# Expert results added by the scatter into a running sum, and values projected per row block

## The chip, the cores and the metric

The kernel runs on one core of a Trainium2 chip. The metric is the device time of one execution in microseconds (us). The core has five engines that run their own instruction streams and meet at semaphores: PE (TensorE, matrix products), DVE (VectorE), ACT (ScalarE), POOL (GpSimd) and SP (SyncE, which here only issues DMAs). The profile lists PE's weight loads apart, as PEld. Sixteen DMA engines carry the transfers that the engines issue.

## What is computed

x has 8 batches of 512 rows of 256 numbers (float32). After a layernorm, two results are added to x:

```python
xn = _layernorm(x)                       # over the 256 columns, no scale
x = x + attention(xn) + ffn(xn)

# attention: 16 heads of 16, windows of 128 rows, stride 64; their outputs stand one
# behind the other and are cut to 512 rows, so four windows (320 rows) per batch count
qkv = xn @ w_qkv + b_qkv
ow = softmax(qw @ kw.T / 4) @ vw         # per window and head
o = ow.reshape(b, nw * 128, 256) @ w_out + b_out
return o[:, :512, :]

# ffn: each row goes to the 2 of 8 experts with the highest scores
topk_scores, topk_idx = top_k(xn @ gate_w.T, 2)
topk_probs = softmax(topk_scores)        # the row's two shares
h12 = xn @ w12[e].T
y = sum over the two experts of  share * ((silu(h1) * h2) @ w3[e].T)
```

## The kernel before

**Stages.** Times are those of the trace. From 0 to 53 x is loaded (L375, four DMAs), normalised into XN and stored to `xn_scratch` in DRAM (`store_xn`, L381), and transposed; the gates' scores and batch 0's projections are made. From 53 to 157.5 attention runs for batches 0 and 1 (EXTRA = 2), and beside it the routing: which row goes to which slot of which expert, and its two shares, kept in PW. From 157.5 to 513.5 the experts run over 71 tiles of 128 slots (SLOT_TILES). From 513.5 to the end attention runs for batches 2 to 7.

**Attention.** A batch has four windows of two units each, u = 0 to 7; a unit is 8 heads of one window. The work is pipelined over units. Each unit on PE: projections for the next batch (queries and keys of a row block in u = 0 to 3, into W_BANK; values of window n = u - 4 in u = 4 to 7, by `values`), the scores three units ahead, the `shifted` scores (L1399: KS by QALL, 8 products of 128x128 for 8 heads, in two halves of 4), `weighted` sums with VW, and every second unit `project`. ACT copies projections out of the bank (`take_part`, `take_values` L741, one copy of 128x256 per window), makes the exponentials (`exps`, L781), copies a row of shifts (`take_shift`, L776) and every second unit the window's sums and denominators (`sides`, L788, L789). DVE splits queries and keys into three bf16 levels, finds maxima (L964), takes the reciprocal of the denominators (L1122, once per window) and adds in `project` (L1132). POOL multiplies (`divide`, L595). SP stores the levels to `parts_scratch` and loads them in another layout (QS, KS); `begin(b)` holds these DMAs of a batch. XNT holds the next batch's transposed rows, loaded by `load_tokens`.

**Experts.** For a tile j POOL gathers 128 rows of `xn_scratch` (`gather`, L654, an indirect DMA into one of two buffers XS), PE transposes them (`tokens`, L1527) and multiplies, ACT copies the result YS (`take_y`, L893), and POOL scatters it to `ys_scratch`, a row of its own for each (token, choice) pair (`scatter`, L658). The weights lie in WALL, 384 KB per DMA (`load_experts`, L449, 4 DMAs per expert); those of experts 6 and 7 (LATE = 6) come last, when the slot map is done, and PE's and ACT's expert programs begin behind a wait for them (`late_in`, L899, L1520).

**Putting together.** After the experts WALL is free. Rows of x (`in_x`, XR) and the two results of each row (YG) are loaded batch by batch (`rest`, 1.5 MB in three DMAs); ACT multiplies each result by its share (`scale`, L796, 64 in all) and POOL adds three terms per tile of 128 rows (`combine`, L601 to L603). For batches 3 to 7 that is done for the batch at hand (`own`), ahead of `divide`, and `project` adds the sum instead of the bias; for batches 2, 0 and 1 it is done later, within batches 4, 5 and 6 (`later`), and `send_later` stores them. Batches 0 and 1's attention output waits in DRAM meanwhile (`keep`, L481, `rows_scratch`).

The order of all engines' work is written out by hand in loops over batches and units; nothing is scheduled by a planner. `c["W"]` and its like count the uses of a bank.

## Time and profile before

| | us |
|---|---|
| median of 3 runs | 712.34 |
| lowest, highest | 712.1, 715.86 |
| the profiled execution | 713.24 |
| its span, from the first to the last instruction | 711.5 |

The profile is of one execution. A line "busy" names engines by the time they execute something; PE's share includes pipelined matrix products whose ends are modelled. The chain of waits is followed back from the last instruction: at each step to what released it. Since the stages have different limits, a view of a stretch or of one engine's timeline tells more than the averages over the span.

### The profile page before, as it was taken

The numbers are of one execution on the slowest core, as the hardware profiler recorded it, in microseconds if no ns is written. First come the engines' busy times: TensorE is split into PE (matmuls) and PEld (weight loads), VectorE is DVE, ScalarE is ACT, GpSimd is POOL, SyncE is SP. The second block draws the span as 40 slices with busy tenths as digits, with TensorE's granted clock in tenths as the row PEclk, the third lists the DMA queues.
The fourth block names the chain that finished last, engine by engine and source line by source line (L and its number), as shares of the span: only waits on it lengthen the run. The fifth ranks groups of instructions, "written<-read, shape, count | busy, mean of one in ns | idle before, by whom it ended". The sixth has DMA issues, their size and how long they took to land.

```text
span 711.5 us, 17988 instructions
## 1 busy us (share of the span) xinstructions
PE 633.2 (89%) x5916; PEld 512.0 (72%) x5917; DVE 571.6 (80%) x906; ACT 513.7 (72%) x883; POOL 280.4 (39%) x330
## 2 busy tenths in 40 slices
PE   0786776978999999999999999999889899999995
PEld 0564554754888888888888888888767676666673
DVE  4958899975688888888888888888687979788884
ACT  4554477474687787787777777777667788888885
POOL 3000273031344444444444444444300336666654
PEclk9998788998999999999999999999999999999999
DMA  9895477581111111111111111112168687885840
GB/s 300 268 257 174 128 262 273 146 284 31 49 53 52 59 52 52 59 53 50 59 55 50 57 56 51 56 54 56 45 161 258 174 259 180 271 227 161 215 138 30
DMA packets 66384, 92.74 MB, mean 130 GB/s; under 512 B 6448, under 2 KB 53424, under 8 KB 66320
## 3 DMA queue, kind: packets, MB, share of 16 engines
q1 hardware_dynamic: 57904, 70.56, 33.3%
q0 software_dynamic: 6864, 18.75, 7.9%
q10 hardware_dynamic: 1568, 2.76, 1.2%
q8 instruction: 32, 0.52, 0.3%
q14 instruction: 16, 0.13, 0.1%
HBM read 59.06 MB, written 32.83 MB: 129 GB/s over the span
## 4 chain that ended last, share of the span: by engine, by line
PE 63%; DVE 14%; ACT 10%; issue 8%; DMA 2%; POOL 2%; ACTq 0%; SPq 0%; DVEq 0%; POOLq 0%
PE PS L1300 55%; PE PS L1549 4%; DVE SMALL L964 4%; ACT WORK L781 3%; DVE XN L1122 2%; PE PS L1527 2%; DVE WALL L958 2%; ACT QS L776 1%; DMA XN<-in_x 1%; DVE WORK L1033 1%; DVE WORK L1026 1%; POOL OTS L595 1%; ACT WORK L719 1%; DVE WALL L982 1%; DMA KS<-parts_scratch 1%
## 5 line engine op out<-in xcount | busy, mean ns | idle before, releaser
L367 DVE TENSOR_TENSOR WS<-WALL,WS 128x1024 fp32r<-128x1024 f32 x136 | 166.9, 1227 | 56.0 <-ACT WS L862 41.5
L1300 PE MATMUL PS<-WS,XTS 128*128 128x512 f32 x804 | 203.9, 402 | 0.0
L1300 PEld LDWEIGHTS PS<-WS,XTS 128*128 128x128 f32 x804 | 146.2, 189 | 30.5
L862 ACT ACTIVATE WS<-WALL 128x1024 fp32r x136 | 143.7, 1056 | 9.1 <-issue 0.3
L1300 PE MATMUL PS<-DOWN_HIGH,HTS 128*128 x568 | 108.3, 290 | 5.0 <-DVE DOWN_LOW L958 3.5
L595 POOL TENSOR_TENSOR OTS<-SIDE,XN 128x256 f32<-128x256 f32 x31 | 23.8, 768 | 209.2 <-DVE XN L1122 142.2
L1300 PEld LDWEIGHTS PS<-DOWN_HIGH,HTS 128*128 128x128 f32 x568 | 86.4, 190 | 5.5 <-issue 5.5
L964 DVE TENSOR_REDUCE SMALL<-PS 128x8 f32<-128x1024 f32 x64 | 77.5, 1211 | 12.6 <-PE PS L1300 12.4
L781 ACT ACTIVATE WORK<-PS 128x512 f32<-128x512 f32 x128 | 69.4, 594 | 24.8 <-PE PS L1300 21.4
L658 POOL DMA_INDIRECT ys_scratch<-SIDE,SIDX x36 | 43.8, 1215 | 97.0 <-ACT SIDE L893 97.0
L654 POOL DMA_INDIRECT XS<-xn_scratch,GIDX x72 | 70.4, 978 | 23.6 <-issue 21.6
L1300 PE MATMUL PS<-DOWN_LOW,HTS 128*128 x284 | 79.5, 280 | 0.0
L658 POOL DMA_INDIRECT ys_scratch<-OTS,SIDX x35 | 45.0, 1286 | 81.6 <-ACT OTS L893 81.6
L776 ACT ACTIVATE QS<-PS 16x1024 bf16<-16x1024 bf16 x64 | 65.1, 1017 | 3.4 <-PE PS L1396 1.9
L1300 PEld LDWEIGHTS PS<-KS,QS 96*128 96x128 bf16 x512 | 33.1, 101 | 31.5 <-DVE SMALL L964 24.2
L958 DVE TENSOR_TENSOR HTS<-PS,HTS 128x512 fp32r<-128x512 f32 x71 | 49.1, 692 | 7.2 <-ACT HTS L877 7.2
L1122 DVE RECIPROCAL XN<-XN 128x256 f32<-128x256 f32 x31 | 54.1, 1746 | 0.0
L1300 PEld LDWEIGHTS PS<-DOWN_LOW,HTS 128*128 128x128 f32 x284 | 53.9, 190 | 0.0
L1300 PE MATMUL PS<-KS,QS 96*128 96x128 bf16 x512 | 41.1, 225 | 12.6 <-DVE SMALL L964 12.3
L958 DVE TENSOR_TENSOR WORK<-WORK,PS 128x512 f32<-128x512 f32 x71 | 48.4, 681 | 3.9 <-PE PS L1300 3.9
L1300 PE MATMUL PS<-WORK,VW 128*32 128x128 f32 x1024 | 42.6, 285 | 5.2 <-ACT WORK L781 5.2
L1300 PE MATMUL PS<-WOUT,OTS 128*128 128x256 f32 x128 | 36.1, 405 | 11.7 <-POOL OTS L595 9.5
(148 smaller groups left out, 1094.8 us busy)
## 6 DMA issues: line engine op xcount, KB each, us to landing
WALL<-in_wexp SPq DMA_DIRECT2D x28, 384.0 KB, 7.1
WALL<-ys_scratch SPq DMA_DIRECT2D x16, 512.0 KB, 7.3
parts_scratch<-WORK SPq DMA_DIRECT2D x32, 240.0 KB, 2.5
QS<-parts_scratch SPq DMA_DIRECT2D x16, 480.0 KB, 4.6
XN<-in_x SPq DMA_DIRECT2D x4, 1024.0 KB, 12.1
xn_scratch<-XN SPq DMA_DIRECT2D x4, 1024.0 KB, 7.2
WALL<-in_x SPq DMA_DIRECT2D x8, 512.0 KB, 5.7
KS<-parts_scratch SPq DMA_DIRECT2D x16, 240.0 KB, 3.9
```

The lines of the kernel that those rows point to most:

```text
L367: eng.tensor_tensor(out=WS[:, 1 - k, half, 1], in0=weights, in1=WS[:, 1 - k, half, 0].bitcast(F32), op=ALU.subtract).then_inc(low_ready[ha ...
L595: pool.tensor_tensor(out=OTS[:].rearrange("p c n -> p (c n)"), in0=SIDE[:], in1=DENS, op=ALU.mult).then_inc(turned_ready, 1)
L654: pool.indirect_dma_start(XS[:, j % 2, :], None, xn_dram, bass.IndirectOffsetOnAxis(GIDX[:, j:j + 1], 0)).then_inc(xs_in[j % 2], 16)
L658: pool.indirect_dma_start(ys_dram, bass.IndirectOffsetOnAxis(SIDX[:, j:j + 1], 0), YS[j % 2], None).then_inc(y_out[j % 2], 16)
L776: act.activation(to, SHIFT_ROW.unsqueeze(1).to_broadcast([2 * HH, HH, WIN]), ACT.Copy).then_inc(t_free, 1)
L781: act.activation(PT[:, 2 * (u % 2) + q, :], ST_BANK[q], ACT.Exp, scale=SCALE).then_inc(probs_ready, 1)
L862: act.activation(WS[:, 1 - k, half, 0], weights, ACT.Copy).then_inc(high_ready[half], 1)
L958: return dve.tensor_tensor(out=o, in0=a, in1=b, op=op)
L964: return dve.tensor_reduce(out=o, in_=a, axis=AX_X, op=op, **kw)
L1122: dve.reciprocal(out=DENS, in_=DENS).then_inc(recip_ready, 1)
L1300: return pe.matmul(o, a, b, start=start, stop=stop)
L1549: last = pe.transpose(bank(6)[:, f * P:(f + 1) * P], HID[:, k, f * P:(f + 1) * P], IDF[:])
```

## The change

**Shares.** PW is laid out [128, 32, 2], and after making it DVE signals `shares_made`. ACT, in batch 0 at u = 5, stores it into two new columns of `xn_scratch`, whose rows now have 258 numbers. A gather so brings a row's two shares along; `take_map` makes a mask KIND (which of the two a slot is), and POOL picks the share by two small operations (`find_share`), two tiles ahead. `take_y` multiplies by it in its copy.

**The sum.** `sum_scratch` starts as a copy of x, made by eight DRAM-to-DRAM DMAs (`copy_x`): two behind the first loads of experts' weights, six ahead of the late ones. `scatter` adds to it, and each waits for the scatter before; the first waits for all copies. `keep` adds batches 0 and 1's attention output to it from POOL. After the experts `rest` loads 0.5 MB per batch; `own` adds the bias only, for all batches from 2 on; `scale`, `later`, `rows_back` and `send_later` are gone. Batches 0 and 1 go from `sum_scratch` to the output in two DMAs.

**Values.** They are projected once for row blocks of 128, 128 and 64 rows in u = 4, 5, 6 (the last into T_BANK); ACT copies them in six pieces to the four windows' places. Odd windows then hold their keys' rows with the halves swapped, so `shifted` of an odd window puts its two halves by two products of 64 columns.

```diff
+VBLOCKS = -(-SPAN // P)
+BLOCK_USES = 4 + VBLOCKS
+VTAKES = (((0, 0, P), (1, STRIDE, P)), ((2, 0, P), (1, 0, STRIDE)), ((3, STRIDE, P),), ((3, 0, STRIDE),))
...
+        xn_dram = nc.dram_tensor("xn_scratch", (B * L, ROW), F32, kind="Internal").ap()
+        sum_dram = nc.dram_tensor("sum_scratch", (DUMP_ROW + SLOT_TILES * P, D), F32, kind="Internal").ap()
...
+            def copy_x(b):
+                r = slice(b * L, (b + 1) * L)
+                sp.dma_start(sum_dram[r], x[r]).then_inc(x_copied[b], 16)
 
             def rest(b):
-
                 t = slice(b * TB, (b + 1) * TB)
-                sp.dma_start(XR[:, t, :], xv[:, t, :]).then_inc(rest_in[b], 16)
-                for k in range(2):
-                    sp.dma_start(YG[:, t, k, :], yv[:, t, k, :]).then_inc(rest_in[b], 16)
-
-            def rows_back(b):
-                t = slice(b * TB, (b + 1) * TB)
-                sp.dma_start(XN[:, t, :], rv[:, t, :]).then_inc(rows_in[b], 16)
-                rest(b)
+                sp.dma_start(XR[:, t, :], sv[:, t, :]).then_inc(rest_in[b], 16)
...
-            def keep(b):
-                sp.wait_ge(r_free, (b + 1) * NWIN + 1)
-                t = slice(b * TB, (b + 1) * TB)
-                sp.dma_start(rv[:, t, :], XN[:, t, :]).then_inc(rows_out, 16)
-
             begin(0)
             load_experts(FIRST_EXPERTS, EARLY - 1)
+            for b in range(EXTRA):
+                copy_x(b)
             sp.wait_ge(early_done, 1)
             load_tokens(1)
             load_experts(EARLY - 1, LATE)
             begin(1)
+            for b in range(EXTRA, B):
+                copy_x(b)
             sp.wait_ge(map_done, 1)
             load_experts(LATE, E)
-            keep(0)
-            load_tokens(2)
-            keep(1)
-            sp.wait_ge(rows_out, 16 * EXTRA)
+            load_tokens(EXTRA)
...
             for b in range(EXTRA, LAST):
                 begin(b)
                 rest(b + 1)
                 if b < LAST - 1:
                     load_tokens(b + 1)
-                if b + 2 in LATER:
-                    if LATER[b + 2] < EXTRA:
-                        rows_back(LATER[b + 2])
-                    else:
-                        rest(LATER[b + 2])
-                if b > OWN:
+                if b == EXTRA:
+                    for src in range(EXTRA):
+                        r = slice(src * L, (src + 1) * L)
+                        sp.dma_start(out[r], sum_dram[r]).then_inc(out_done, 16)
+                else:
                     send(b - 1)
...
-            def combine(t, first, ready):
-
-                total = XR[:, t, :]
-                link(pool.tensor_tensor(out=total, in0=total, in1=first, op=ALU.add))
-                link(pool.tensor_tensor(out=total, in0=total, in1=YG[:, t, 0, :], op=ALU.add))
-                pool.tensor_tensor(out=total, in0=total, in1=YG[:, t, 1, :], op=ALU.add).then_inc(ready, 1)
+            def keep(b):
+
+                pool.wait_ge(r_free, (b + 1) * NWIN + 1)
+                pool.wait_ge(x_copied[b], 16)
+                t = slice(b * TB, (b + 1) * TB)
+                pool.dma_start(sum_dram[0:B * L].rearrange("(t p) d -> p t d", p=P)[:, t, :], XN[:, t, :],
+                               accum_op=ALU.add).then_inc(rows_out[b], 16)
 
             def own(b, n):
-                pool.wait_ge(own_scaled, 2 * ((b - OWN) * TB + n + 1))
-                pool.wait_ge(rest_in[b], 48)
-                combine(b * TB + n, BOUT[:], own_ready)
-
-            def later(b, n):
-
-                pool.wait_ge(later_scaled, 2 * ((b - FIRST_LATER) * TB + n + 1))
-                src = LATER[b]
-                pool.wait_ge(rest_in[src], 48)
-                if src < EXTRA:
-                    pool.wait_ge(rows_in[src], 16)
-                else:
-                    pool.wait_ge(r_free, src * NWIN + n + 2)
-                combine(src * TB + n, XN[:, src * TB + n, :], later_ready)
+                pool.wait_ge(rest_in[b], 16)
+                t = b * TB + n
+                pool.tensor_tensor(out=XR[:, t, :], in0=XR[:, t, :], in1=BOUT[:], op=ALU.add).then_inc(own_ready, 1)
...
+            keep(0)
 
             def gather(j):
                 pool.indirect_dma_start(XS[:, j % 2, :], None, xn_dram,
                                         bass.IndirectOffsetOnAxis(GIDX[:, j:j + 1], 0)).then_inc(xs_in[j % 2], 16)
 
             def scatter(j):
-                pool.indirect_dma_start(ys_dram, bass.IndirectOffsetOnAxis(SIDX[:, j:j + 1], 0),
-                                        YS[j % 2], None).then_inc(y_out[j % 2], 16)
+                if j:
+                    pool.wait_ge(y_out[1 - j % 2], 16 * ((j + 1) // 2))
+                else:
+                    for b in range(B):
+                        pool.wait_ge(x_copied[b], 16)
+                    for b in range(EXTRA):
+                        pool.wait_ge(rows_out[b], 16)
+                pool.indirect_dma_start(sum_dram, bass.IndirectOffsetOnAxis(SIDX[:, j:j + 1], 0),
+                                        YS[j % 2], None, compute_op=ALU.add).then_inc(y_out[j % 2], 16)
+
+            def find_share(j):
+                k = j % 2
+                pool.wait_ge(xs_in[k], 16 * (j // 2 + 1))
+                link(pool.tensor_tensor(out=PAIR[:], in0=XS[:, k, D:ROW], in1=KIND[:, j, :], op=ALU.mult))
+                pool.tensor_tensor(out=SHARE[:, k:k + 1], in0=PAIR[:, 0:1], in1=PAIR[:, 1:2], op=ALU.add
+                                   ).then_inc(share_ready, 1)
+                pool.wait_ge(share_ready, j + 1)
 
             pool.wait_ge(map_done, 1)
             for blk in range(4):
                 pool.wait_ge(parts_out[blk], PARTS_OUT[blk // 2] * (EXTRA + 1))
+            pool.wait_ge(shares_out, 16)
             gather(0)
             gather(1)
             divide(6)
             divide(7)
+            find_share(0)
+            find_share(1)
             pool.wait_ge(xt_full, 1)
             gather(2)
...
+            keep(1)
             for j in range(SLOT_TILES):
                 if j + 3 < XS_TILES:
                     pool.wait_ge(xt_full, j + 2)
                     gather(j + 3)
                 pool.wait_ge(ys_ready, j + 2)
                 scatter(j)
+                if j + 2 < SLOT_TILES:
+                    find_share(j + 2)
...
-                    if b in LATER:
-                        later(b, n)
-                    if b >= OWN:
-                        own(b, n)
+                    own(b, n)
                     if b * NWIN + n < B * NWIN - 1:
...
-            def take_values(n, bk, full, ready):
+            def take_values(i, bk, full, ready):
                 act.wait_ge(full[0], full[1])
-                act.activation(values_of(n), values_in(bk), ACT.Copy).then_inc(ready, 1)
+                for n, lo, hi in VTAKES[i]:
+                    last = act.activation(values_of(n)[lo:hi], values_in(bk)[lo:hi], ACT.Copy)
+                last.then_inc(ready, 1)
...
-                    elif not last and u < UNITS - 1:
-                        take_values(u - 4, W_BANK[:, 0:D], (w_full, c["W"].add()), w_free)
-                    if b in LATER and u % 2 == 0:
-                        scale(LATER[b] * TB + u // 2, LATER[b], later_scaled)
-                    if b >= OWN and u % 2 == 1:
-                        scale(b * TB + u // 2, b, own_scaled)
+                    elif not last and u == 4:
+                        take_values(0, W_BANK[:, 0:D], (w_full, c["W"].add()), w_free)
+                    elif not last and u == UNITS - 2:
+                        take_values(1, W_BANK[:, 0:D], (w_full, c["W"].add()), block_taken)
                     if b == 0 and u == 1:
                         act.wait_ge(gap_ready, 2)
                         act.activation(E2, PA, ACT.Exp).then_inc(e2_ready, 1)
                         act.wait_ge(xn_out, 64)
+                    if b == 0 and u == 5:
+                        act.wait_ge(shares_made, 1)
+                        act.dma_start(xn_dram.rearrange("(t p) d -> p t d", p=P)[:, :, D:ROW], PW[:]
+                                      ).then_inc(shares_out, 16)
                     if u % 2 == 1:
                         if b == EXTRA and u == 1:
                             act.wait_ge(y_stored, 1)
                         sides()
                     if u == UNITS - 1 and not last:
-                        take_values(NWIN - 1, W_BANK[:, 0:D], (w_full, c["W"].add()), w_free)
+                        take_values(2, W_BANK[:, 0:D], (w_full, c["W"].now()), w_free)
+                        take_values(3, T_BANK[:, 0:D], (w_full, c["W"].add()), w_free)
...
-                    act.activation(YS[k], bank(7)[:, 0:D], ACT.Copy).then_inc(ys_ready, 1)
+                    act.wait_ge(share_ready, j + 1)
+                    act.activation(YS[k], bank(7)[:, 0:D], ACT.Copy, scale=SHARE[:, k:k + 1]).then_inc(ys_ready, 1)
...
-                link(ts(MB, hi, float(NT), float(B * L), ALU.is_gt, ALU.mult))
-                link(tt(MB, MA, MB, ALU.subtract))
+                link(ts(KIND[:, :, 0], hi, float(NT), None, ALU.is_le, ALU.bypass))
+                link(ts(KIND[:, :, 1], hi, float(NT), None, ALU.is_gt, ALU.bypass))
+                link(dve.scalar_tensor_tensor(out=MB, in0=KIND[:, :, 1], scalar=-float(B * L), in1=MA, op0=ALU.mult,
+                                              op1=ALU.add))
...
+                rows = min(P, SPAN - n * P)
                 for ch in range(NC_D):
-                    last = mm(o, xt[:, ch, n * STRIDE:n * STRIDE + WIN], WQKV[:, ch, 2 * D:3 * D],
+                    last = mm(o[0:rows], xt[:, ch, n * P:n * P + rows], WQKV[:, ch, 2 * D:3 * D],
                               ch == 0, ch == NC_D - 1)
...
-                        last = mm(o, KS[:, par, half * HH + h, w], QALL[0:DEEP, par, half * HH + h, w])
+                        moving = QALL[0:DEEP, par, half * HH + h, w]
+                        if n % 2 == 0:
+                            last = mm(o, KS[:, par, half * HH + h, w], moving)
+                        else:
+                            for part in range(2):
+                                at = (n + 1 - part) * STRIDE
+                                last = mm(o[part * STRIDE:(part + 1) * STRIDE],
+                                          KS[:, par, half * HH + h, at:at + STRIDE], moving)
```

ACT's order in batch 0, around the operations of u = 5. Before:

```order
L808 ACTIVATE XN<-XN,WALL 128x512 [waits apart]
L776 ACTIVATE QS<-PS 16x8x128 [waits t_full]
L743 ACTIVATE VW<-PS 128x2x8x16 [waits w_full]
L788 ACTIVATE SIDE<-PS 128x256 [waits turned_ready,o_full]
L789 ACTIVATE XN<-PS 128x256
L781 ACTIVATE WORK<-PS 128x512 [waits sides_ready,st_full]
```

and now:

```order
L796 ACTIVATE XN<-XN,WALL 128x512 [waits apart]
L769 ACTIVATE QS<-PS 16x8x128 [waits t_full]
L815 DMA xn_scratch<-PW 128x32x2 [waits shares_made]
L781 ACTIVATE SIDE<-PS 128x256 [waits turned_ready,o_full]
L782 ACTIVATE XN<-PS 128x256
L774 ACTIVATE WORK<-PS 128x512 [waits sides_ready,st_full]
```

The DMA of PW stands between `take_shift` and `sides`.

SP's order from the end of batch 1's loads to the expert tiles. Before, the late weights follow the last KS loads directly, with the stores of `keep` behind them:

```order
L412 DMA KS<-parts_scratch 48x2560 [waits parts_out3]
L412 DMA KS<-parts_scratch 32x2560
L412 DMA KS<-parts_scratch 16x2560
L449 DMA WALL<-in_wexp 128x768 [waits map_done]
L449 DMA WALL<-in_wexp 128x768 x7
L481 DMA rows_scratch<-XN 128x4x256 [waits r_free]
L429 DMA WORK<-xt_scratch 128x640 [waits w_full]
L481 DMA rows_scratch<-XN 128x4x256 [waits r_free]
```

and now:

```order
L410 DMA KS<-parts_scratch 48x2560 [waits parts_out3]
L410 DMA KS<-parts_scratch 32x2560
L410 DMA KS<-parts_scratch 16x2560
L451 DMA sum_scratch<-in_x 16x8192 x6
L447 DMA WALL<-in_wexp 128x768 [waits map_done]
L447 DMA WALL<-in_wexp 128x768 x7
L427 DMA WORK<-xt_scratch 128x640 [waits w_full]
```

Six copies stand ahead of the late weights, and `keep` has left SP.

POOL's order at the start of the expert tiles. Before (L595 is `divide`, L654 `gather`, L658 `scatter`):

```order
L654 DMA XS<-xn_scratch,GIDX 128x256 [waits parts_out2,parts_out1,parts_out3,parts_out0,map_done]
L654 DMA XS<-xn_scratch,GIDX 128x256
L595 TENSOR_TENSOR OTS<-SIDE,XN 128x256 [waits r_full,recip_ready,sides_ready] x2
L654 DMA XS<-xn_scratch,GIDX 128x256 [waits xt_full] x2
L658 DMA ys_scratch<-SIDE,SIDX 17280x256 [waits ys_ready]
L654 DMA XS<-xn_scratch,GIDX 128x256 [waits xt_full]
L658 DMA ys_scratch<-OTS,SIDX 17280x256 [waits ys_ready]
L654 DMA XS<-xn_scratch,GIDX 128x256 [waits xt_full]
```

and now (L577 is `divide`, L585 `keep`, L627 `gather`, L638 `scatter`, L644 and L645 `find_share`):

```order
L585 DMA sum_scratch<-XN 128x4x256 [waits x_copied0,r_free]
L627 DMA XS<-xn_scratch,GIDX 128x258 [waits parts_out2,parts_out3,parts_out1,shares_out,parts_out0,map_done]
L627 DMA XS<-xn_scratch,GIDX 128x258
L577 TENSOR_TENSOR OTS<-SIDE,XN 128x256 [waits r_full,recip_ready,sides_ready] x2
L644 TENSOR_TENSOR PAIR<-XS,KIND 128x2 [waits xs_in0]
L645 TENSOR_TENSOR SHARE<-PAIR 128x1 [waits pool_step]
L644 TENSOR_TENSOR PAIR<-XS,KIND 128x2 [waits xs_in1,share_ready]
L645 TENSOR_TENSOR SHARE<-PAIR 128x1 [waits pool_step]
L627 DMA XS<-xn_scratch,GIDX 128x258 [waits xt_full,share_ready]
L585 DMA sum_scratch<-XN 128x4x256 [waits x_copied1,r_free]
L627 DMA XS<-xn_scratch,GIDX 128x258 [waits xt_full]
L638 DMA sum_scratch<-SIDE,SIDX 13184x256 [waits x_copied5,x_copied4,x_copied6,x_copied3,x_copied7,x_copied2,rows_out0,x_copied1,rows_out1,x_copied0,ys_ready]
```

Accumulating stores and the shares' operations have come between the gathers, and a scatter now waits for the one before.

## Rows read from the trace of the kernel before

**Rows 1.** The page: busy time (part 1) and shares of the chain of waits (part 4)

```profile
PE 633.2 (89%) x5916; PEld 512.0 (72%) x5917; DVE 571.6 (80%) x906; ACT 513.7 (72%) x883; POOL 280.4 (39%) x330
...
PE 63%; DVE 14%; ACT 10%; issue 8%; DMA 2%; POOL 2%; ACTq 0%; SPq 0%; DVEq 0%; POOLq 0%
```

**Rows 2.** Stretches: us, busy us (operations) by engine, granted clock, DMA share, GB/s

```profile
105.00:107.00 2.00, 0.95 (x10) 0.79 (x11) 2.00 (x3) 1.86 (x4) 2.00 (x4) 1.00 1.04 340
145.00:149.00 4.00, 4.00 (x59) 3.23 (x58) 2.27 (x5) 2.93 (x6) 1.31 (x2) 1.00 1.02 393
153.00:155.00 2.00, 0.00 (x0) 0.00 (x0) 1.98 (x2) 1.96 (x3) 0.00 (x0) 1.00 1.02 378
200.00:250.00 50.00, 50.00 (x311) 43.85 (x309) 41.73 (x52) 38.79 (x63) 23.29 (x21) 1.00 0.15 52
```

**Rows 3.** The load of x at the start: four DMAs of 1024 pieces

```profile
L375 SPq DMA_DIRECT2D XN<-in_x x4: 441/2160/4292, 0.8 to 6.3; - x4
...
DMA to landing us min/median/max: 9.1/12.1/14.0
```

**Rows 4.** Last two late expert loads, issued at 144.5 and 145.0: time to landing

```profile
DMA to landing us min/median/max: 8.6/9.3/10.1
```

**Rows 5.** Chain of waits, batch 1 into expert tiles: start, length, operation

```profile
156.28 1.15 PE PS L1300 x4
...
157.47 0.53 PE PS L1527 x2
```

**Rows 6.** Costliest groups: busy us, mean ns | idle before, its releaser

```profile
L1300 PE MATMUL PS<-DOWN_HIGH,HTS 128*128 x568 | 108.3, 290 | 5.0 <-DVE DOWN_LOW L958 3.5
```

**Rows 7.** POOL in the expert loop: start, length, operation, idle before it

```profile
302.34 1.27 POOL L658 DMA_INDIRECT ys_scratch<-SIDE,SIDX  x1 [2.31 <-ACT SIDE L893]
303.91 0.97 POOL L654 DMA_INDIRECT XS<-xn_scratch,GIDX  x1 [0.30 <-issue]
...
308.76 0.97 POOL L654 DMA_INDIRECT XS<-xn_scratch,GIDX  x1 [0.30 <-issue]
```

**Rows 8.** Scatters of expert results from 300 to 313: issue to landing

```profile
DMA to landing us min/median/max: 2.4/2.7/2.7
```

**Rows 9.** DVE in batch 2

```profile
527.16 1.75 DVE L1122 RECIPROCAL XN<-XN 128x256 f32<-128x256 f32 x1
...
529.98 0.49 DVE L958 TENSOR_TENSOR WORK<-WORK 128x320 bf16<-128x320 f32 x1
...
533.94 1.75 DVE L1122 RECIPROCAL XN<-XN 128x256 f32<-128x256 f32 x1
```

**Rows 10.** DVE in batch 3

```profile
550.69 1.75 DVE L1122 RECIPROCAL XN<-XN 128x256 f32<-128x256 f32 x1
...
559.82 1.75 DVE L1122 RECIPROCAL XN<-XN 128x256 f32<-128x256 f32 x1
...
562.64 0.90 DVE L958 TENSOR_TENSOR WORK<-WORK 128x320 bf16<-128x320 f32 x1
...
567.01 1.74 DVE L1122 RECIPROCAL XN<-XN 128x256 f32<-128x256 f32 x1
```

**Rows 11.** DVE in batch 4: its first three reciprocals

```profile
584.01 1.75 DVE L1122 RECIPROCAL XN<-XN 128x256 f32<-128x256 f32 x1
...
593.60 1.75 DVE L1122 RECIPROCAL XN<-XN 128x256 f32<-128x256 f32 x1
...
601.20 1.75 DVE L1122 RECIPROCAL XN<-XN 128x256 f32<-128x256 f32 x1
```

**Rows 12.** ACT in the last unit of batch 2: the copy of values

```profile
544.75 0.38 ACT L743 ACTIVATE VW<-PS 128x256 f32<-128x256 f32 x1
```

**Rows 13.** PE's weight loads in batch 3, last window: a DMA wait

```profile
572.21 0.45 PEld L1300 LDWEIGHTS PS<-KS,QS 96*128 96x128 bf16 x8 [0.39 <-DMA KS<-parts_scratch]
```

**Rows 14.** ACT's scaling of loaded expert results, all of it

```profile
L796 ACT ACTIVATE WALL<-WALL,PW x64: 491/497/510, 551.1 to 703.9; 128x256 f32<-128x256 f32 x64
```

**Rows 15.** Chain of waits from 680 to the end: its shares by line

```profile
by line: ACT WORK L781 26.9%; PE PS L1300 24.8%; ACT QS L776 9.5%; issue 8.9%; ACT WALL L796 5.6%; ACT SIDE L788 4.8%; DVE XN L1130 3.9%; ACT XN L789 3.5%; DVE XN L958 2.2%; ACT VW L743 1.2%; ACTq L791 0.2%; DVEq L1137 0.1%
```

83 lines of the change are left out of this document (36 added, 47 removed).

## The prediction

> **What bounds the kernel now.** I read the page first [rows 1]. PE is busy 89% of the span and leads the chain of waits with 63%, but that is an average over stages with different limits. So the second view is the table of stretches [rows 2], and within a stage the timelines. In the expert tiles (157.5 to 513.5) PE is busy 50.00 of 50.00 us at full clock [rows 2] and everything else has room: POOL idles 2.31 us before a scatter [rows 7]. One tile takes 4.85 us (gathers at 303.91 and 308.76 [rows 7]). In attention batch 0 it is ACT and DVE: 1.86 and 2.00 of 2 us busy while PE works 0.95, in the stretch from 105 to 107 [rows 2]. From batch 2 on a chain through all engines sets the pace, window by window; its beat is read from the starts of L1122 on DVE [rows 9 to 11]. Between these stages stands one transfer, the late experts' weights: from 145 to 155 the DMA engines are full (1.02 shares, 378 to 393 GB/s [rows 2]).
>
> The sum is made on the profiled execution, 713.24 us for a span of 711.5; it lies 0.9 above the median 712.34, which comes off at the end. Edits within 0.5% (3.6 us) are about what a measurement of this kernel can tell from none.
>
> **The six copies ahead of the late weights.** Before, the last two late loads were issued at 144.5 and 145.0 and landed 8.6 and 10.1 us later [rows 4], so at 155.1. PE ends batch 1 at 157.43 and starts its first expert operation at 157.47 [rows 5]; that operation's sequencer waits for all late weights first, which cost nothing with 2.4 us to spare. Now six copies of x (3.15 MB) are issued on SP before those loads. At the 378 to 393 GB/s that the engines carry there [rows 2] they take 8.0 to 8.3 us, so the weights land at about 163.3 and PE starts 5.8 us late. Above that stands keep(0): issued behind the weights before, it may now be served ahead of them, 0.52 MB or 1.3 us, so 7.1. If DRAM-to-DRAM pieces move at half that rate it is 14; if the engines serve both queues side by side and copies finish last, below zero is excluded and it may be 0. I take **+6.5**. PE's start passes on whole: what follows is PE's own work, then its 3.5 us wait for DVE's DOWN_LOW [rows 6], and DVE makes those after `hidden(0)`, which needs PE. Nothing that batch 1 gains before this point survives it.
>
> **The shares' way out.** ACT, in batch 0's unit 5 (near 105), now issues one DMA of 4096 pieces of 8 bytes (128 x 32). No such DMA is in the trace. The nearest rows are the loads of x: four issues of 1024 pieces [rows 3]; the first two go in at once (0.44 and about 0.6 us), one takes 4.29, and each lands within 14.0 us of its issue. I read it as a queue that takes some 2000 pieces and holds the issuing engine for the rest until pieces have drained. Here half of 4096, so 128 on each of 16 engines, must drain with ACT held. With 1 KB pieces the queue moved 4096 of them in some 12 us, 256 per engine, so 47 ns for each. What 8 bytes take lies between nothing and that; I take a little over half, 27 ns, since some of the 47 must be fixed: 128 x 27 = **+3.5**. ACT stands on the limiting chain here [rows 2], so it counts whole. The lower end is 0.4 (the cheapest issue [rows 3]); the upper end follows if the pieces take turns with the early expert weights, with the engines at 1.04 shares from 105 on [rows 2]: then 128 pieces at 47 ns plus as much for each neighbour, 12 us.
> The Trainium skill, "DMA: Bandwidth & Descriptors", Specifications, says that below 512 B the DMA engine does a read-modify-write; it speaks against 8-byte shares, and by it the hold would lie nearer the upper end, the sum some 8 us higher. No row here has such small pieces.
>
> **The map.** `take_map` does 8 DVE operations for 7; the nearest row is an addition of 0.49 us on a tile four times as wide [rows 9], at least 0.1 remains: **+0.2**, on batch 1's DVE chain, partly absorbed by the wait above.
>
> **Expert tiles.** POOL gets two tiny operations per tile and `take_y` a wait for them. POOL idles 2.31 us per tile before the scatter [rows 7] and the shares are found two tiles ahead, so PE stays the limit. The scale itself rides on an ACT operation that is there anyway. New is the scatter's wait for the one before: issue to landing is 2.4 to 2.7 us for plain stores [rows 8]. An accumulating one must also read 128 KB; at one more transfer of that size (a gather's own length, 0.97 us of issue [rows 7] and about as much of flight) I estimate 3.5 to 4.3 us from issue to landing. That is under the period of 4.85, by 0.5 to 1.3. So **0**, with POOL's `gather(j+4)` queued behind the scatter's wait but not needed for a whole tile. The 8 bytes more in a gathered row of 1 KB cost nothing, since the gather is three tiles ahead.
> The Trainium skill, "DMA: Bandwidth & Descriptors", section "Anatomy of one DMA — SWDGE (gpsimd) path", gives 2.0 us fixed and the bytes at 436 GB/s, 2.3 us for 128 KB; the trace's 2.4 to 2.7 agrees. By it a second pass over the bytes adds only 0.3, and the wait would never bind; nothing in the sum changes.
>
> **Values.** Three row blocks replace four windows on PE. In batches 0 to 6 PE has four 128x256 products fewer in unit 7, none of them on the limiting chain, and ACT makes six copies for four. The copies: full ones take 0.38 us each [rows 12]. In batch 0 ACT limits: three more operations among the units (one partial) give 2 to 3 x 0.35, **+1.0**; in batch 1 it is absorbed. In batches 2 to 6 unit 7 has one more copy on the way sides, values, exps, shift, part, DVE: +0.33 each, below. The odd windows' `shifted` doubles its products (8 more of 64 columns per half). Eight weight loads take 0.45 us [rows 13], and PE waits 0.39 us there for KS from DRAM anyway, so 0 to 0.1. If halves in different columns run side by side, 0.
> The Trainium skill, "TensorEngine Tiling (Array Packing)", Key Properties, has tiles load weights and multiply in parallel; by that it is 0, by the row alone at most 0.45 in the two last units, 0.5 us per batch if DMA ceased to be late.
>
> **Stage 2, batches 2 to 7.** ACT's 64 scalings (0.497 us [rows 14]) go, and POOL adds one tile for three. From the reciprocals: window 0 to 1 takes 9.13 in batch 3 [rows 10] and 9.59 in batch 4 [rows 11], window 1 to 2 takes 6.78 in batch 2 [rows 9], 7.19 in batch 3, 7.60 in batch 4 (and in 5 and 6). The difference is contention of POOL's additions with DVE: one WORK addition takes 0.49 in batch 2 and 0.90 in batch 3 [rows 9, 10]. After, `own` runs once, right behind `divide`, in all batches from 2 on. So batch 2 rises to 7.19 (+0.41) and gets the copy (+0.33): +0.74. Batch 3: +0.33. Batches 4 and 5: -0.46 - 0.41 + 0.33 = -0.54 each. Batch 6 the same without most of the copy's charge, since batch 7 has no values to take: -0.87. In batch 7 ACT limits; L796 has 5.6% of the chain's last 32 us [rows 15], 1.8 us, of which the next limit (PE, 24.8%) takes back a little: -1.5. Sum 0.74 + 0.33 - 1.08 - 0.87 - 1.5 = **-2.4**. Bounds: +1 if nothing but batch 7 gains, -8 if contention leaves altogether. The loads fall from 1.5 MB to 0.5 MB per batch; none was waited for.
>
> **The sum.** 713.24 + 6.5 + 3.5 + 0.2 + 0 + 1.0 - 2.4 = 722.04; less 0.9: **721.1 us**.
>
> **The rivals.**
> - *Shares' issue is cheap* (0.4): 718.0. For it: the two first loads issued in 0.44 and 0.6 [rows 3]. Against: twice as many pieces as these together.
> - *Shares held among the expert loads* (12 us): 729.6. For it: DMA 1.04 busy from 105 [rows 2].
> - *The accumulating scatter is slower than a tile*: from 4.85 us on each of 71 tiles waits for the one before; at 5.5 it is 71 x 0.65 = 46 us, so 767. Against: 2.4 to 2.7 now [rows 8].
> - *The other side, faster*: ACT's scalings were on stage 2's path more than the chain of one execution tells. They are 64 x 0.497 = 32 us busy [rows 14]. The costs come to 11.2, so the kernel is faster by over 0.5% once more than 14.7 us of these 32 come back; at 19, it is 704.5. Against: ACT idles in most units there, and DVE's share of the beat doesn't change.
> - *The change's cost does not appear*: the copies are served beside the weights (0) and the issue is cheap (0.4): 713.24 + 1.6 - 2.4 - 0.9 = 711.5, no difference.
>
> **How the numbers follow.** Forecast 0.42 (716 to 726), cheap issue 0.15, held long 0.12, slow scatter 0.08, faster 0.13, no cost 0.10. Faster 0.13, same 0.14, slower 0.73, since a part of the cheap issue's range reaches under 715.9. For 8 in 10 the range leaves out the slow scatter and most of the faster case: 707 to 734.
>
> **What would show it.** In the changed profile: PE's first L1527 near 164 with a wait for a WALL load; ACT's DMA at L815 with 3 to 5 us between its neighbours; 4.85 us between gathers, and scatters landing under it; the second interval of batch 2 at 7.2, batch 4's first at 9.1; in batch 7 no L796. It would be wrong if scatters land later than 4.85, or if stage 2 sheds far more than 2.4.

## The result and the profile after

The changed kernel takes 728.8 us (median of 4 runs, 727.0 to 730.1) where the kernel before took 713.4 (four runs beside it, 712.1 to 715.9). The ratio is 1.021, with a 95% interval from 1.017 to 1.025: slower, by 1.7 to 2.5%. The forecast was 721.1 with a range of 707 to 734. The profiled execution has 729.2 us and a span of 727.5, 16.0 more than the 711.5 of before, and the rest of this text accounts for these 16.0.

The page of the changed kernel, busy times and the chain's shares; they answer to [rows 1]:

```profile
PE 636.5 (87%) x6140; PEld 507.8 (70%) x6141; DVE 569.2 (78%) x907; ACT 496.3 (68%) x835; POOL 346.0 (48%) x402
...
PE 59%; DVE 15%; ACT 10%; DMA 7%; issue 5%; POOL 3%; SPq 2%; ACTq 0%; DVEq 0%; POOLq 0%
```

PE has 3.3 us more to do and ACT 17 less, and yet the span grew: in the chain DMA rose from 2% to 7%. Where, the timelines tell. Set beside each other at five points of the program and at its end they give this table (starts of the same operation, us):

| | before | after | added in the stretch |
|---|---|---|---|
| DVE's last reciprocal of batch 1 | 153.36 | 153.69 | 0.3 |
| PE's first expert operation | 157.47 | 167.29 | 9.5 |
| ACT's copy of the first expert result | 173.98 | 183.89 | 0.1 |
| ACT's copy of the last (71st) expert result | 513.28 | 526.88 | 3.7 |
| DVE's first reciprocal of batch 2 | 527.16 | 540.75 | 0.0 |
| end of the span | 711.5 | 727.5 | 2.4 |

**The wait for the late weights.** The chain of waits of the changed kernel from 150 to 182; it answers to [rows 5]:

```profile
151.06 15.78 DMA WALL<-in_wexp
...
167.29 0.67 PE PS L1532 x2
```

The last load of the late experts' weights was issued at 151.06 and landed 15.8 us later. Before, the last one was issued at 145.0 and took 10.1 [rows 4]. Ahead of the weights the issue of the six copies held SP for 5.0 us, from 141.96 on.

**The shares' way out.** ACT's one DMA of 4096 pieces, from the view of its line:

```profile
L815 ACTq DMA_DIRECT2D xn_scratch<-PW x1: 393/393/393, 94.6 to 94.6; - x1
...
DMA to landing us min/median/max: 26.7/26.7/26.7
```

Its issue took 0.39 us; nothing was held. It stood at 94.6, not near 105 as the prediction read it. It landed 26.7 us later, and nobody waited for that.

**The expert tiles.** POOL's timeline in the loop (start, length, operation, idle before it); it answers to [rows 7]:

```profile
220.90 1.60 POOL L638 DMA_INDIRECT sum_scratch<-OTS,SIDX  x1 [0.30 <-issue]
221.96 1.56 POOL L644 TENSOR_TENSOR PAIR<-XS,KIND 128x2 f32<-128x2 f32 x1
223.61 0.19 POOL L645 TENSOR_TENSOR SHARE<-PAIR 128x1 f32<-128x1 f32 x1
224.30 1.00 POOL L627 DMA_INDIRECT XS<-xn_scratch,GIDX  x1 [0.49 <-POOL SHARE L645]
225.66 1.69 POOL L638 DMA_INDIRECT sum_scratch<-SIDE,SIDX  x1 [0.36 <-ACT SIDE L885]
```

POOL was idle for 2.3 us ahead of each scatter [rows 7]; now the gaps are 0.3 to 0.7 us, and POOL is busy for 39.9 of the 50 us from 200 to 250, where it was 23.3 [rows 2]. (The records of a scatter and of PAIR behind it overlap by some 0.5 us, so these lengths are rough.) The product PAIR of two columns takes 1.6 us here, but 0.20 where POOL is otherwise idle (at 162.0). The end of the loop on POOL:

```profile
524.51 1.58 POOL L638 DMA_INDIRECT sum_scratch<-OTS,SIDX  x1 [2.53 <-ACT OTS L885]
529.09 1.55 POOL L638 DMA_INDIRECT sum_scratch<-SIDE,SIDX  x1 [2.99 <-DMA sum_scratch<-OTS,SIDX]
```

The last scatter waited 2.99 us for the one before, which so took 4.6 us from issue to landing. Plain ones took 2.4 to 2.7 [rows 8].

**Attention from batch 2.** The reciprocals, as in [rows 9 to 11]. The first four here are those of batch 2's four windows (the last of them runs in batch 3's part of the program):

```profile
540.75 1.75 DVE L1116 RECIPROCAL XN<-XN 128x256 f32<-128x256 f32 x1
...
547.93 1.74 DVE L1116 RECIPROCAL XN<-XN 128x256 f32<-128x256 f32 x1
...
557.77 1.75 DVE L1116 RECIPROCAL XN<-XN 128x256 f32<-128x256 f32 x1
...
568.10 1.74 DVE L1116 RECIPROCAL XN<-XN 128x256 f32<-128x256 f32 x1
...
577.23 1.74 DVE L1116 RECIPROCAL XN<-XN 128x256 f32<-128x256 f32 x1
...
584.41 1.75 DVE L1116 RECIPROCAL XN<-XN 128x256 f32<-128x256 f32 x1
```

The steps are 7.18, 9.84, 10.33, 9.13 and 7.18. Before they were 6.78, 7.32, 9.43, 9.13 and 7.19. So batch 2 lost 3.8 us: 0.4, 2.5 and 0.9 in its three steps. In the step of 9.84 PE waits for KS from DRAM (timeline of its weight loads; it answers to [rows 13]):

```profile
555.50 0.45 PEld L1296 LDWEIGHTS PS<-KS,QS 96*128 96x128 bf16 x8 [2.65 <-DMA KS<-parts_scratch]
```

The step behind it has a part that belongs to no operation. From 557.1 to 560.5, right behind this wait, PE's granted clock is at its lower level, 1.2 GHz; from 530 to 557.1 and from 560.5 on it is 1.00. The row gives stretch, busy us (operations) by engine, granted clock, DMA share and GB/s:

```profile
557.10:560.50 3.40, 3.40 (x53) 2.83 (x53) 3.33 (x5) 2.10 (x3) 0.84 (x2) 0.50 0.40 159
```

The kernel before has no such stretch from batch 2 on until its last microsecond. In the profiled executions below with the same attention code, this third step is 10.2 to 10.3 where a stretch of 3.4 us at the lower clock lies at its start or just ahead of it (three others, with second steps of 9.9 to 10.9), and 9.8 where none does (four, with second steps of 7.8 to 8.9). Without the values part the second step is as long, 9.87, the clock stays at 1.00, and the third step is 9.43, as in that kernel's other batches. So I put 0.5 of the 0.9 down to the clock and 0.4 to the step's own work; no run sets the clock by itself.

From the reciprocal at 568.10 on, the changed kernel takes 159.4 us, before 160.8: here it gains 1.4.

### The profile page after: what moved, and what is told of

Its sections match the earlier page's. It is cut to its first block, busy times and chain, and to the rows that moved or that the text cites. A ratio compares the mean times of both kernels' runs of the same rounds, so it can differ in the third digit from the quotient of the medians.

```text
span 727.5 us, 18605 instructions
## 1 busy us (share of the span) xinstructions
PE 636.5 (87%) x6140; PEld 507.8 (70%) x6141; DVE 569.2 (78%) x907; ACT 496.3 (68%) x835; POOL 346.0 (48%) x402
## 4 chain that ended last, share of the span: by engine, by line
PE 59%; DVE 15%; ACT 10%; DMA 7%; issue 5%; POOL 3%; SPq 2%; ACTq 0%; DVEq 0%; POOLq 0%
PE PS L1296 52%; PE PS L1554 4%; DVE SMALL L957 4%; DVE XN L1116 3%; ACT WORK L774 2%; PE PS L1532 2%; DMA WALL<-in_wexp 2%; DVE WALL L951 2%; DMA KS<-parts_scratch 1%; DMA XN<-in_x 1%; DMA parts_scratch<-WORK 1%; ACT QS L769 1%; DVE WORK L1026 1%; DMA XS<-xn_scratch,GIDX 1%; DVE WORK L1019 1%
## 5 line engine op out<-in xcount | busy, mean ns | idle before, releaser
L577 POOL TENSOR_TENSOR OTS<-SIDE,XN 128x256 f32<-128x256 f32 x31 | 23.8, 768 | 259.9 <-DVE XN L1116 247.2
L1296 PE MATMUL PS<-DOWN_HIGH,HTS 128*128 x568 | 110.3, 293 | 5.0 <-DVE DOWN_LOW L951 3.5
L644 POOL TENSOR_TENSOR PAIR<-XS,KIND 128x2 f32<-128x2 f32 x71 | 108.0, 1522 | 5.8 <-DMA XS<-xn_scratch,GIDX 5.8
L627 POOL DMA_INDIRECT XS<-xn_scratch,GIDX x72 | 72.8, 1011 | 41.1 <-POOL SHARE L645 34.8
L638 POOL DMA_INDIRECT sum_scratch<-SIDE,SIDX x36 | 59.7, 1660 | 29.9 <-ACT SIDE L885 25.6
L638 POOL DMA_INDIRECT sum_scratch<-OTS,SIDX x35 | 58.3, 1665 | 18.1 <-ACT OTS L885 16.1
```

The source lines that it names most:

```text
L627: pool.indirect_dma_start(XS[:, j % 2, :], None, xn_dram, bass.IndirectOffsetOnAxis(GIDX[:, j:j + 1], 0)).then_inc(xs_in[j % 2], 16)
L638: pool.indirect_dma_start(sum_dram, bass.IndirectOffsetOnAxis(SIDX[:, j:j + 1], 0), YS[j % 2], None, compute_op=ALU.add).then_inc(y_out[j ...
L644: link(pool.tensor_tensor(out=PAIR[:], in0=XS[:, k, D:ROW], in1=KIND[:, j, :], op=ALU.mult))
L1296: return pe.matmul(o, a, b, start=start, stop=stop)
```

## The experiments

All were compared with the kernel before on the same chip, which took 712.8 to 713.7 there; the changed kernel was not run beside them, so differences to its 728.8 are good to about 1 us. Where a span or a step is told, it is that of the profiled execution. Profiled starts of the same point differ by up to 2.1 us between kernels that are alike up to there (the first reciprocal at 77.1 to 79.1), so stretches are better compared than starts.

### The copies and the accumulating store

The first two kernels move one of two suspects each, the third both.

Copies behind the late weights:

```diff
-            for b in range(EXTRA, B):
-                copy_x(b)
             sp.wait_ge(map_done, 1)
             load_experts(LATE, E)
+            for b in range(EXTRA, B):
+                copy_x(b)
```

> The changed kernel with its six copies of x issued behind the late experts' weights instead of ahead of them. The changed kernel's PE starts its first expert operation at 167.3 us, 9.8 later than before. Theory: 5.8 of these are the six copies (8.2 us of transfer less 2.4 of slack) and 4 are the accumulating store of batch 0's rows, which shares the queues' time with the weights. Then this kernel starts the experts near 158 to 161 (the accumulating store is still in the way) and takes about 7 to 9 us less than the changed kernel, 720 to 722. Rival: only the copies cost, moving at half the rate of a load, and the accumulating store nothing: start at 157.8, 719. If the wait was not what the copies caused, the time stays at 728 to 729.

Measured: 725.9 us, ratio 1.017 (1.014 to 1.020), 2.9 under the changed kernel and not the 7 to 9 expected. The weights are no longer what PE waits for, yet its first expert operation starts at 161.9 and the second pair at 165.0 (PE's weight loads):

```profile
161.91 0.29 PEld L1532 LDWEIGHTS PS<-IDF,XS 128*128 128x128 f32 x2 [3.02 <-issue]
165.00 0.29 PEld L1532 LDWEIGHTS PS<-IDF,XS 128*128 128x128 f32 x2 [2.79 <-DMA XS<-xn_scratch,GIDX]
```

The wait is now for the gathers. They stand on POOL's queue behind the accumulating store of batch 0's rows, issued at 145.1 and landed at 159.9; the second gather was on its way for 16.6 us (chain of waits), where the gathers of before took 6.2 and 6.6 beside the same weights:

```profile
148.38 16.57 DMA XS<-xn_scratch,GIDX
```

Whether the store delays them by its place in the queue or by its traffic, no run tells apart.

The store moved, the copies left where they are:

```diff
             for w in range(3, 6):
                 divide(w)
-            keep(0)
...
             gather(2)
+            keep(0)
             keep(1)
```

> The changed kernel with batch 0's accumulating store moved on POOL from ahead of the first gather to behind the third, beside batch 1's. Theory (the store takes 4 of the 9.8 us): PE's first expert operation at about 163.3 and the kernel at 724 to 725. Rival (the copies alone cost, at half rate): still at 167 and 728 to 729.

Measured: 724.9, ratio 1.015 (1.011 to 1.018), as expected; the four runs lie from 722.8 to 728.5, and the profiled one is the slowest of them. PE starts the experts at 165.15, 2.1 earlier than in the changed kernel, half of what the theory gave the store:

```profile
151.57 13.13 DMA WALL<-in_wexp
...
165.15 0.68 PE PS L1532 x2
```

Both moves:

> Both moves at once: copies behind the late weights, batch 0's accumulating store behind the third gather. Both theories: PE's first expert operation at 157.8 as before the change, and 719 to 720. If moving them only shifts the cost (first scatter waits for the copies, exact part of the experts waits for the stores), the experts' first results come late: ACT's first result after 175, and 722 or more.

Measured: 721.5, ratio 1.011 (1.008 to 1.015), span 718.7, between the theory's 719 to 720 and the rival's 722. PE's first expert operation is back at its old place:

```profile
157.47 1.12 PE L1532 MATMUL PS<-IDF,XS 128*128 128x128 f32 x4
```

So the 9.8 us are the copies and the store together. With the store alone moved 7.7 us of wait remain, with the copies alone moved 4.5, and only both moves free PE. (Counted from batch 1's last reciprocal, which comes 0.5 and 0.9 us later in these two profiles than in the changed kernel, it is 6.8 and 3.2 of 9.5.) The first expert result comes at 181.8 and 181.5 in these two, against 174.0 before; with the copies alone moved, PE waits again, until 165.0, for the second gather.

Of the 9.8 us, 8.5 arrive at the first expert result (16.5 us after PE's start before, 17.9 here). The other 1.4 lie on PE: ahead of the first products with DOWN_HIGH it reads the tile's expert number from EJ, and this one read took 1.67 us where it took 0.31 before. DVE's DOWN_LOW was ready as early as before (170.2). PE's reads from 165 to 176, before and here (ns, min/median/max):

```profile
L1578 PEldq TENSOR_LOAD <-EJ x3: 297/301/313, 170.3 to 173.6; - x3
...
L1583 PEldq TENSOR_LOAD <-EJ x3: 301/301/1667, 170.2 to 175.0; - x3
```

Why it was slow once, no run shows. And PE's granted clock was at its lower level for 6.8 us from 171.2 on, 2.6 of them behind the first result, where before it was 3.4 and 0.8. That lengthens the step to the second result, 6.87 us here, 5.93 before and 6.16 in the changed kernel. Over all fourteen profiled executions this step grows with the time at the lower clock in it, from 5.56 with none to 6.87 with 2.6 us, by 0.5 us for each.

### The values

Undone in the changed kernel (four products and copies per batch, undivided products in odd windows):

```diff
-                    elif not last and u == 4:
-                        take_values(0, W_BANK[:, 0:D], (w_full, c["W"].add()), w_free)
-                    elif not last and u == UNITS - 2:
-                        take_values(1, W_BANK[:, 0:D], (w_full, c["W"].add()), block_taken)
+                    elif not last and u < UNITS - 1:
+                        take_values(u - 4, W_BANK[:, 0:D], (w_full, c["W"].add()), w_free)
...
-                        if n % 2 == 0:
-                            last = mm(o, KS[:, par, half * HH + h, w], moving)
-                        else:
-                            for part in range(2):
-                                at = (n + 1 - part) * STRIDE
-                                last = mm(o[part * STRIDE:(part + 1) * STRIDE],
-                                          KS[:, par, half * HH + h, at:at + STRIDE], moving)
+                        last = mm(o, KS[:, par, half * HH + h, w], QALL[0:DEEP, par, half * HH + h, w])
```

> The changed kernel with values projected per window again (four products, four copies, undivided products in the odd windows), all else as changed. Theory: the values part costs one ACT copy in each of the seventh units of batches 2 to 6, +0.33 each, and 0.1 in one interval per batch; undone it gives 2 us back, 726 to 727, and the longest interval between reciprocals falls from 9.80 to 9.45. Rival: PE's doubled small products cost more, up to 0.9 per odd unit pair, 4 to 5 us in all: 724. Other rival: projecting three blocks helps PE and undoing it loses 1: 730.

Measured: 724.6, ratio 1.016 (1.013 to 1.019), 4.2 under the changed kernel. From the first reciprocal of batch 2 to the end it takes 183.2 us, the changed kernel 186.7. Two steps of each batch are shorter, 9.80 became 9.42, and 7.58 became 7.32, so the small products cost more than the theory gave them, as the first rival has it, though not 0.9. (0.5 of the 3.5 us is batch 2's third step, where the clock didn't fall here.) DVE's reciprocals:

```profile
582.16 1.74 DVE L1108 RECIPROCAL XN<-XN 128x256 f32<-128x256 f32 x1
...
589.48 1.74 DVE L1108 RECIPROCAL XN<-XN 128x256 f32<-128x256 f32 x1
...
598.90 1.75 DVE L1108 RECIPROCAL XN<-XN 128x256 f32<-128x256 f32 x1
```

The values part alone, in the kernel before:

> The kernel before with only the values part of the change (three row blocks, six copies, divided products in odd windows). Undoing this part in the changed kernel gave 4 us back (728.8 to 724.6; by the intervals between reciprocals 0.38 in one and 0.26 in another of each batch). Theory: it costs the same alone, +2.5 to +4: 715.5 to 717.5. Rival: in the kernel before ACT's scalings already delay unit 7, so the additional copy is hidden, and only the divided products show: +1 or less, 714.

Measured: 717.1 against 713.1, ratio 1.0048 (1.0031 to 1.0066), 4.0 us by the medians; span 715.9, +4.4. The theory holds and the rival falls: the additional copy isn't hidden by ACT's scalings. The steps from a batch's third to its fourth reciprocal, 9.43 to 9.52 before, became 9.81 to 9.94.

One more thing showed in the kernel without the values part. The step between the third and fourth reciprocal of the kernel is 13.95 us there, 12.56 in the changed one and before. PE waits for batch 1's rows (weight loads):

```profile
109.03 0.44 PEld L1288 LDWEIGHTS PS<-WORK,WQKV 128*128 128x128 f32 x2 [2.90 <-DMA WORK<-xt_scratch]
```

With per-window values PE is done with the rows of the batch before one unit later, so their load is issued later, and two copies of x then stand ahead of it. The values part made room for copies that the sum part brought.

### The expert loop

Both kernels of this part compute something else. The first leaves out POOL's two operations that find a share, from the third tile on, and scales with the first two tiles' shares:

```diff
                 scatter(j)
-                if j + 2 < SLOT_TILES:
-                    find_share(j + 2)
...
-                    act.wait_ge(share_ready, j + 1)
```

> The changed kernel with the two POOL operations that find a tile's share left out from the third tile on; results are scaled by the first two tiles' shares, so each row's experts are weighted wrongly. In the changed kernel ACT's results run from 183.9 to 526.9, 343.0 us for 70 tiles, before 339.3; in the last seven tiles PE waits 0.2 to 0.7 for a gather. Theory: these two operations (1.6 and 0.2 us, the first waiting for DVE's hold of the memory port) fill POOL's tile, gathers come late in the last tiles and every second tile is 0.08 longer. Without them 339.5 to 340.5 and 3 us less, 725 to 726. Rival: the accumulating scatter's traffic slows PE's weight loads and its wait delays the gathers: 343 stays, 728 to 729.

The second stores where the changed kernel adds, with all waits kept:

```diff
-                                        YS[j % 2], None, compute_op=ALU.add).then_inc(y_out[j % 2], 16)
+                                        YS[j % 2], None).then_inc(y_out[j % 2], 16)
```

> The changed kernel with the scatter storing plainly instead of adding (a row keeps the last result written, so the sums are wrong); its waits stay. Theory: an adding scatter takes about 4.6 us to landing (seen for the last but one, 524.51 to 529.09), a plain one 2.7; the loop doesn't feel it, 343 us from first to last result as in the changed kernel, but the last scatter no longer waits 3.0 us, the experts' end comes 3 to 4 us earlier for SP, and the second interval between reciprocals in batch 2 falls from 9.84 towards 7.6 to 8: 725 to 727. Rival: the adding scatter is what lengthens the loop: 340 us and 723 or less.

Measured: 727.5 (ratio 1.020, 1.017 to 1.024) and 725.5 (1.017, 1.015 to 1.020). What the loop did, from the starts of ACT's copies of the results:

| kernel | first to last result | mean of tiles 10 to 60 | last seven full tiles |
|---|---|---|---|
| before | 339.3 | 4.840 | 33.79 |
| changed | 343.0 | 4.873 | 35.21 |
| shares left out | 342.4 | 4.873 | 34.03 |
| plain scatter | 341.1 | 4.873 | 33.98 |
| values undone | 342.7 | 4.873 | 34.82 |
| values alone | 339.2 | 4.840 | 33.80 |

Two parts must be told apart. The last seven tiles lose 1.2 us because gathers come late; that is POOL's doing, and either experiment takes it away. PE's waits from 488 to 527 in the changed kernel (us in total, times, longest); in the two others there is no such row on XS:

```profile
PEld PS L1532 <- DMA XS<-xn_scratch,GIDX: 2.2, 5, 0.7
```

The other part, 0.033 us per tile or 2.3 in all, is untouched by both and by the values: neither theory nor rival holds for it. It lies in PE's own products of the second layer (costliest groups from 200 to 500, before and after):

```profile
L1300 PE MATMUL PS<-DOWN_HIGH,HTS 128*128 x496 | 93.6, 288 | 0.0
...
L1300 PE MATMUL PS<-DOWN_LOW,HTS 128*128 x248 | 68.9, 278 | 0.0
```

```profile
L1296 PE MATMUL PS<-DOWN_HIGH,HTS 128*128 x490 | 94.4, 291 | 0.0
...
L1296 PE MATMUL PS<-DOWN_LOW,HTS 128*128 x245 | 68.9, 281 | 0.0
```

Twelve of them at about 3 ns more make up the 0.033; the clock is 1.00 in both. The traces narrow the cause. The products' lengths come in two patterns, and both kernels have both. The kernel before runs its fourth and fifth tile in the longer one, 4.87 us apart, and stays in the shorter one, at 4.84, from the sixth on. The changed kernel has the shorter one in its third tile and again in tiles 66, 67 and 70, where gathers come late, and the longer one in nearly all others. Before from 188.5 to 198.2 and from 198.2 to 500, then changed from 506.1 to 508 (ns, min/median/max):

```profile
L1300 PE MATMUL PS<-DOWN_LOW,HTS x8: 281/281/283, 188.9 to 194.8; 128*128 x8
...
L1300 PE MATMUL PS<-DOWN_LOW,HTS x252: 276/277/282, 198.6 to 499.7; 128*128 x126
...
L1296 PE MATMUL PS<-DOWN_LOW,HTS x4: 276/278/280, 506.5 to 507.5; 128*128 x4
```

So gathered rows of 1032 bytes and another place in memory are not enough to lengthen a product: these three tiles have both. What decides in which pattern a loop stays is open.

The plain scatter's span is 4.9 us shorter: 0.3 ahead of the first result, 1.9 in the experts (1.2 in the last tiles, 0.6 ahead of the second result) and 2.7 behind them. Of these, the 0.6 and another 0.5 us in batch 2's third step are places where the clock was at its lower level in the changed kernel and not here. No run sets the clock by itself, so what brought that about is open. POOL at the end of its loop (compare the 2.99 us of wait above):

```profile
522.36 0.99 POOL L638 DMA_INDIRECT sum_scratch<-OTS,SIDX  x1 [3.65 <-ACT OTS L885]
525.51 0.96 POOL L638 DMA_INDIRECT sum_scratch<-SIDE,SIDX  x1 [2.17 <-ACT SIDE L885]
```

The last scatter waits only for its data, and the second step of batch 2 is 7.84 instead of 9.84. Where the shares are left out, the last tiles give their 1.2 back too, but that step is 10.88, and the kernel gains only 1.3 us by the medians, not the 3 expected.

### Who makes batch 2 wait

```diff
-                    outs(b + 1, half)
+                    if b != EXTRA or half:
+                        outs(b + 1, half)
...
+            sp.wait_ge(probs_ready, 2 * UNITS * EXTRA + 2)
+            outs(EXTRA + 1, 0)
             sp.wait_ge(y_stored, 1)
```

> The changed kernel with SP issuing the first half of batch 3's stores ahead of its wait for the last scatter, instead of behind it. Theory: batch 2's long second interval (9.84 against 7.32 before; PE waits 2.65 us for KS) comes from SP standing at that wait 3 us longer than before, so that the stores bunch with the next loads. Here it falls to 7.6 to 8 and the time by 2, 726 to 727. Rival: the transfers themselves (rows of the sum loaded by SP at the same time) are the cause: 9.8 stays, 728 to 729.

Measured: 728.3 (ratio 1.020, 1.018 to 1.023), only 0.5 less, within what runs differ by. The step fell to 8.69, not to 7.6 to 8: the first stores ahead of the wait give 1.15 us of the 2.5. (The third step fell too, from 10.33 to 9.82; the clock stayed at 1.00.) SP in the changed kernel:

```profile
533.13 0.56 SPq L486 DMA_DIRECT2D KS<-KS  x1
533.73 0.58 SPq L455 DMA_DIRECT2D WALL<-sum_scratch  x1
534.41 2.24 SPq L394 DMA_DIRECT2D parts_scratch<-WORK  x3
...
544.49 0.36 SPq L398 DMA_DIRECT2D parts_scratch<-WORK  x1
...
548.89 2.23 SPq L410 DMA_DIRECT2D KS<-parts_scratch  x3
```

SP stands until 533.13 for the last scatter (6.25 us after the last result; before 3.2: 513.28 to 516.47). Its stores then bunch with the loads that follow, and the one issued at 544.49 takes 4.4 us to land. With the plain scatter, SP is free 3 us earlier and the step is 7.84; so the cause is the accumulating scatter's late end, of which the order on SP passes on a part.

### Versions that were meant to be faster

All four repairs at once (copies and store behind, values undone, stores first; the edits are those shown above):

> The changed kernel with the copies behind the late weights, batch 0's accumulating store behind the third gather, values as before the change, and batch 3's first stores ahead of SP's wait. If the four repairs add up: 728.8 - 7.3 - 3.8 - 2 = 715.7, still 3 above the kernel before, the rest being the experts' stage. If the last overlaps with the first (batch 2's interval is already shorter without the copies), 717.

Measured: 717.8 against 713.7, ratio 1.0061 (1.0043 to 1.0080). The experts' stage still costs 3.1 us, the wait for batch 1's rows 1.8.

The share moved from ACT's copy to a product on DVE, alone in the changed kernel, to test what lengthens the tile:

```diff
-                    act.wait_ge(share_ready, j + 1)
-                    act.activation(YS[k], bank(7)[:, 0:D], ACT.Copy, scale=SHARE[:, k:k + 1]).then_inc(ys_ready, 1)
+                    act.activation(YS[k], bank(7)[:, 0:D], ACT.Copy).then_inc(ys_ready, 1)
...
-                    tt(HID[:, k, :], HID[:, k, :], bank(2 * k + 1), ALU.mult).then_inc(hid_done, 1)
+                    dve.wait_ge(share_ready, j + 1)
+                    dve.scalar_tensor_tensor(out=HID[:, k, :], in0=HID[:, k, :], scalar=SHARE[:, k:k + 1],
+                                             in1=bank(2 * k + 1), op0=ALU.mult, op1=ALU.mult).then_inc(hid_done, 1)
```

> The changed kernel with the share applied on DVE, in the product of the two halves of the hidden layer (a scalar as a third operand of an operation that is there anyway), and ACT's copy of the result unscaled again. The tile takes 4.873 us with or without POOL's share operations or the adding scatter, before 4.840. Theory: ACT's scaled copy (0.475 instead of 0.385 us) holds the result's bank longer and PE's next products in it wait a little every second tile: here 4.840 and 2.3 us less. Rival: rows of 1032 instead of 1024 bytes, or the additional load on memory, slow PE's weight loads: 4.873 stays. If DVE's three-operand form is much slower, the tile grows above 4.88.

Measured: 743.0, ratio 1.041 (1.039 to 1.043). The tile takes 5.13 us, for a reason that no theory had: DVE needs the share a stage earlier than ACT did, and POOL finds it behind the scatter, which waits for the result before. PE, DVE and POOL now stand in one ring (DVE's timeline):

```profile
302.78 0.75 DVE L1247 SCALAR_TENSOR_TENSOR WORK<-WORK,SHARE,PS 128x512 f32<-128x512 f32 x1 [0.44 <-POOL SHARE L645]
```

It doesn't settle the 0.033, since PE was not the limit in it. Both patterns of the products' lengths are mixed throughout its loop (DOWN_LOW 279 ns in the mean), with rows of 1032 bytes and the adding scatter in place. That fits with the theory that ACT's scaled copy has a part in it, but doesn't show it.

> The combined kernel of 717.8 with four further edits: all eight copies of x behind the late weights (two of them stood ahead of the load of batch 1's rows, and the interval from the third to the fourth reciprocal was 14.4 instead of 12.6), both accumulating stores of attention rows behind the fourth gather, the share applied on DVE, and found by one POOL operation (share times sign plus mask) instead of two. If all add up: -1.5, -1.3, -2.3 and -0.7 to -1.4: 711 to 712, 2 under the kernel before. If the scaled copy is not what lengthens the tile, 713.5 to 714.5.

Measured: 723.2, ratio 1.014 (1.012 to 1.016). The share on DVE spoiled it (tile 5.01). Its other edits did what they were for: the step between third and fourth reciprocal is 12.56 again, the first expert result comes at 175.1, and from the last result to the end it takes 194.7 us, where the kernel before takes 198.2.

The last version takes the share back to ACT, finds it ahead of the scatter, and has PE add the bias instead of POOL:

```diff
+                if biased:
+                    mm(R_BANK[:, 0:D], IDF[:], BOUT[:], True, False)
                 pe.wait_ge(turned_ready, c["R"].now() + 1)
```

> The kernel of 723.2 with the share applied again in ACT's copy of the result (applied on DVE, the tile waited for POOL's share and grew to 5.01 us), the share found ahead of the scatter instead of behind it, and POOL's addition of the bias gone from attention: PE adds it, as one more product of the identity with the bias in the projection's bank, ahead of its wait for POOL. Theory: first result at 175.1 as there, tile 4.87 (342 us for the experts), and without POOL's addition the interval from the first to the second reciprocal of a batch falls from 7.19 to 6.78, since DVE then never waits for POOL: 2.5 us over six batches. Sum: 721.0 - 9.0 - 2.5 = 709.5 in the profiled span, 711 to 712 in time, 1 to 2 under the kernel before. Rival: the 7.19 has another cause and stays: 714. If the share ahead of the scatter holds the scatters back, the tile grows: 716 or more.

Measured: 715.1 (11 runs) against 713.2 (16), ratio 1.0029 (1.0013 to 1.0045). The tile is 4.87 and the last tiles have no late gather, but from the first to the last result it takes 343.0 us, not 342: the step from the second to the third is 6.51 where it was 5.47. The step between the first two reciprocals of a batch is 6.78 in batches 2 to 6, as expected, so the 0.41 was POOL's addition against DVE:

```profile
531.08 1.75 DVE L1108 RECIPROCAL XN<-XN 128x256 f32<-128x256 f32 x1
...
533.90 0.49 DVE L943 TENSOR_TENSOR WORK<-WORK 128x320 bf16<-128x320 f32 x1
...
537.86 1.75 DVE L1108 RECIPROCAL XN<-XN 128x256 f32<-128x256 f32 x1
...
546.47 1.75 DVE L1108 RECIPROCAL XN<-XN 128x256 f32<-128x256 f32 x1
```

But the next step grew, from 7.32 (values undone, and in the version before this one) to 7.75, and batch 7's four steps from 23.2 to 24.2 in sum, and they took back more than that: from the first reciprocal of batch 2 to the end it takes 183.0 us, where the version before takes 181.1. PE's additional product is the one edit that adds work there; it was not tried alone. No version here beats the kernel before.

## Why the prediction was right, and where it wasn't

The direction and the place of the largest term were right: it is the wait for the late weights, as said, and 728.8 lies in the range. But it lies outside the 716 to 726 that the forecast itself covers, and in part the errors cancel, which is luck. The nearest number, 729.6, belonged to a rival whose mechanism (ACT held for 12 us by the shares) is not there at all. The sum came to +8.8 on the profiled execution and 16.0 were measured. By its terms:

- **Late weights: +6.5 forecast, 9.5 measured.** The mechanism was right, the size not. The step that failed took the queue's last landing at 163.3 by adding the copies' 8.2 us, at 378 to 393 GB/s, to the landing before, with keep(0) at most 1.3 on top. The store alone cost 2.1, and copies and weights without it landed at 164.7: from 142 to there the engines moved 333 GB/s in the mean (before, 349 from 142 to 155.1). What the step didn't have at all is that an accumulating store holds back the gathers issued behind it on POOL's queue. It is hidden in the changed kernel, since the weights are later still, and shows once they are not (4.5 us of wait).
- **Shares' issue on ACT: +3.5 forecast, 0 measured.** The reading of [rows 3] was wrong: a limit in pieces, taken from loads of 1 KB pieces, doesn't hold for this store. The landing took 26.7 us, but nothing waits for it. The Trainium skill, in "DMA: Bandwidth & Descriptors", Specifications, has the DMA engine do a read-modify-write below 512 bytes. The long landing of the 8-byte pieces doesn't speak against that; that it would hold the engine which issues them was the prediction's own step, and 0.39 us of issue contradict it.
- **Copies in batch 0 and the map: +1.2 forecast, 0.3 measured** at batch 1's last reciprocal. The two copies of x ahead of the load of batch 1's rows have no term; they cost nothing only because of the values part (1.4 us without it), which is luck.
- **Experts: 0 forecast, +3.7 measured.** The rival of the slow scatter didn't come: 4.6 us to landing, just above the estimate of 3.5 to 4.3 and under the period of 4.85. What failed is "POOL idles 2.31 us per tile", counted as room for two tiny operations. An adding scatter costs POOL 1.65 us of its own instead of 1.0 to 1.3, and the operation behind it 1.6 instead of 0.2, so the room was gone, which cost 1.2 us in the last tiles. The 2.3 us of slower products had no term, and why the loop stays in their longer pattern is open. The prediction weighed there the Trainium skill, "DMA: Bandwidth & Descriptors", section "Anatomy of one DMA — SWDGE (gpsimd) path". An estimate from its figures, with the bytes counted twice, is 2.6 us to landing for the adding scatter; the trace has 4.6, and the measurement decides.
- **The end of the experts: not in the sum.** The wait between scatters was priced per tile, where it is hidden, and not for the last one, where it isn't: 3.0 us there, 2.5 of them at the end of the chain in batch 2.
- **Attention from batch 2: -2.4 forecast, +2.4 measured.** The terms by POOL's contention were right to 0.05 (9.59 to 9.14, 7.60 to 7.19, 6.78 to 7.18). The values part was priced at 0.33 and 0 to 0.1 per batch and cost 0.38 and 0.26; PE's small products were not hidden under the 0.39 us of wait for KS [rows 13]. Batch 7 gave 0.4 instead of 1.5: its steps went from 6.55, 6.00, 6.53, 4.88 to 5.90, 7.05, 5.89, 4.74, so that where ACT had no scaling to do, PE's divided products took over; without the values part they are 6.45, 6.10, 6.17, 4.45. The rest is the step of 9.84 and the 0.5 us put down to the lower clock behind it, for which the sum had no term.

So two terms were 4.4 too dear (shares, copies and map) and three 11.6 too cheap (weights 3.0, experts with their start 3.8, attention 4.8).

## What to carry to other kernels

A transfer that is issued ahead of a load with little slack costs its whole length, but look also at what stands behind it on the queue of the engine that issues it: at the first expert result an accumulating store ahead of two gathers cost nearly as much as 3 MB ahead of the weights. A chain of waits between transfers that is hidden in a loop is paid once at the loop's end, where the next stage waits. Where PE has waited, look at the granted clock of the stretch behind before giving the loss to an operation there. And room on an engine is not the idle time of the operations that are there now: measure what the new form of the DMA takes there, with its neighbour.

## What the runs showed of the hardware

- A DMA of 4096 pieces of 8 bytes, issued by ACT: 0.39 us of issue, 26.7 us to landing, and no hold of ACT.
- An indirect scatter of 128 rows of 1 KB takes 4.6 us from issue to landing when it adds (once, without a queue ahead of it), 2.4 to 2.7 when it stores. On POOL it takes 1.65 us instead of 1.0 to 1.3. The POOL operation behind it is lengthened too, whichever it is: PAIR 1.6 us, and without the share's operations the gather 1.6 instead of 0.97 (timeline of the kernel without them):

```profile
301.83 1.72 POOL L638 DMA_INDIRECT sum_scratch<-SIDE,SIDX  x1 [1.25 <-ACT SIDE L882]
303.85 1.60 POOL L627 DMA_INDIRECT XS<-xn_scratch,GIDX  x1 [0.31 <-issue]
```

  With the plain scatter PAIR takes 0.21, but there the gather takes 1.5 in nearly every tile:

```profile
302.70 1.06 POOL L638 DMA_INDIRECT sum_scratch<-SIDE,SIDX  x1 [0.87 <-ACT SIDE L885]
303.79 0.21 POOL L644 TENSOR_TENSOR PAIR<-XS,KIND 128x2 f32<-128x2 f32 x1
...
304.76 1.50 POOL L627 DMA_INDIRECT XS<-xn_scratch,GIDX  x1 [0.49 <-POOL SHARE L645]
```

  DVE is as busy in both (41.7 and 41.8 of the 50 us from 200 to 250), so DVE's hold of a shared memory port (the Trainium skill, "SBUF — State Buffer", section "SBUF: two separate sides") doesn't by itself explain the difference; what does is open.
- POOL's addition of 128x256 next to DVE lengthens DVE's addition from 0.49 to 0.90 us, and 0.41 us of the first step of batches 2 to 6 go when POOL's is gone. This agrees with that page, by which the port is locked for a whole instruction.
- The same products of 128x256 run at 276 or at 281 ns at the same granted clock, in long runs of tiles, and a loop of 4.84 us per tile becomes one of 4.87.
- At PE's lower granted clock, 1.2 GHz, the step from the first to the second expert result takes 0.5 us more for each us of the lower clock in it (5.56 with none, 6.87 with 2.6 us).
- PE's read of one number from EJ takes 0.30 us in the median; it took 1.67 once with both moves, and 1.63 once in the kernel of 723.2.
